# Four groups of an attention and expert block: from a loop with meetings to one list of steps

## The chip, the cores and the metric

The kernel runs on one core of a Trainium2 chip. The metric is the device time of one execution in microseconds. A NeuronCore has a matmul engine (TensorE, PE in the profile; its weight loads are shown as PEld), a vector engine (VectorE, DVE), an activation engine (ScalarE, ACT), a general engine (GpSimd, POOL) and a queue engine that issues transfers (SyncE, SP). They run side by side and wait for one another by semaphores. SBUF is the on-chip memory; PSUM, with eight banks of 128 x 512 floats, takes the results of PE.

## The reference

```python
def reference(x, Wq, bq, Wk, bk, Wv, bv, Wo, bo, gate, w1, w2, w3, c, wmod):   # x is 1 x 2048 x 128
    mod = (_silu(c) @ wmod).reshape(c.shape[0], 6, 1, -1)
    sa, ca, ga, sb, cb, gb = (mod[:, i] for i in range(6))
    ga, gb = (sign * max(abs, 0.25) of each)
    h = _layernorm(x) * (1 + ca) + sa
    x = x + ga * attn(h)     # 16 query heads, 4 key/value heads of 64, rotary, causal softmax, @ Wo + bo
    h = _layernorm(x) * (1 + cb) + sb
    x = x + gb * ffn(h)      # 8 experts 128 -> 512 -> 128, the best two of each token, silu(g) * u
    return x
```

Attention over 2048 tokens falls into four groups, one for each key/value head with its four query heads. The groups write into the same sum and are otherwise alike.

## The kernel before, in words

**Tiling.** The tokens are 16 tiles of 128 and 4 chunks of 512. A pair step J (0 to 7 within a group) is one chunk of queries for two of the four heads; chunk J // 2 sees only keys of chunks up to its own. For each pair step PE computes scores (`s`, L1039, L1041 and the mask L1044), ACT takes exponentials into `full` or, for the diagonal chunk, `diag` (L611, L620), and PE multiplies them with V (`pv`, L1058). The scores have two PSUM banks. Ahead of them the row maxima are found: PE computes scores once more (`max`, L1011, L1014), DVE reduces them (L781, L784, L790), PE transposes the result (`qmax`, L1024) and ACT copies it to QMT (L591). Projections of a tile are `proj` (PE L987, DVE's bias addition L760 and L764, the rotation on POOL L503 to L510), `low` (parts for exact products, ACT L630 to L632, DVE L770, L773) and `qk` (transposes L995, L1001, copies L591). POOL (L472, L481, L485) or DVE (L800, L811) adds up the exponentials of a pair step; its tail is six `sum` pieces (DVE L826 to L833), `rowsum` (PE L1067, DVE L837 to L840), `norm` (DVE L846) and, after each second pair step, `out`, the product with Wo (PE L1076, DVE L853). Everything but the scores and V products goes through a ring of four PSUM banks.

**Order.** All engines walk the same list of steps, in which each does its part. It is made by `group_order`: the scores and V products of the eight pair steps are laid along a line, and the other steps are placed between them by fractions of pair steps. The end of a group's list already holds projections, transposes and maxima of the next group's first two chunks (`next_group`); their values go to V_next. The beginning holds the tail of the last pair step of the group before, `tail_steps(-1)`.

**The loop.** There are three lists: the lead, which prepares group 1; the body, walked three times in a hardware loop (`Fori`); and a closing copy for group 4. All semaphore counts in a list start at zero, so at the end of the lead and of each turn every engine reports to SP (`engine_through`), SP waits for all and for all counts, clears some 20 semaphores and lets them go with `group_go` (L407, L408). The body starts on ACT with a copy of V_next into V (L648). Since the body is one for all groups, the first one has a tail of a group that does not exist: it works on ones and zeros that POOL writes at the start, with an additional slot of zero weights in `wqkv`, `bqkv` and `wo_sb`, and addresses of the group are computed from the loop's register. After the closing copy follow the second norm, the router and the experts (PE L1117, L1131), in hardware loops too.

```python
                for s, count in loop_sems(n):
                    if count:
                        sp.wait_ge(s, count)
                sp.wait_ge(engine_through, 4)
                for s, count in loop_sems(n):
                    if count:
                        sp.sem_clear(s)
                sp.sem_clear(engine_through)
                sp.sem_inc(group_go, 1)
```

Of the kernel before, what the change touches and what calls it, by code (L numbers as in the profile page):

```python
# [33 lines left out]
P = 128  # L34
# [29 lines left out]
def block_kernel(nc, x_in, Wq, bq, Wk, bk, Wv, bv, Wo, bo, gate, w1, w2, w3, c, wmod,  # L64
# [83 lines left out]
    def merge(*placed):  # L148
# [13 lines left out]
        place(tail_steps(-1), 0.02, 1.1), place(diag_steps(7), 8.01, 8.38),  # L162
# [10 lines left out]
    def group_order(*more):  # L173
        return [("values",)] + merge([(float(b), x) for b, x in zip(before, main)], [(begin[end], x) for x in pending],
                                     *side, *more)

    body = group_order(*next_group)
    closing = group_order(place(tail_steps(end - 1), 8.4, 8.9))
# [11 lines left out]

    class Counts:


        def __init__(self, order):
# [9 lines left out]
            for x in order:  # L204
                for key, engine in {
# [7 lines left out]
                                    + (x[0] == "sum" and x[1] not in range(PAIRS) and x[3] == 1)  # L213
# [9 lines left out]

    QUADS = 7
    quad_of, quad_owner = {}, []
    for x in body:
        if x[0] == "s" and x[3] == 0:
            _, J, q, _, m = x
            if q < J // PAIRS or q == 0:
                quad_of[J, m, q] = len(quad_owner)  # L230
                quad_owner.append((J, m, q))

    def acc_quad(J, m):

        J = J % N_J
        return quad_of[J, m, max(J // PAIRS - 1, 0)] % QUADS

    assert len(quad_owner) % QUADS == 0

    with ExitStack() as ctx:  # L240
# [3 lines left out]
        def sem(name):  # L244
# [11 lines left out]
        wqkv = sb("wqkv", [P, GROUPS + 1, QKV])  # L256
        bqkv = sb("bqkv", [P, GROUPS + 1, QKV])
        wo_sb = sb("wo_sb", [P, 1 + GROUPS, PAIRS, E])
# [22 lines left out]
        V = sb("V", [P, TILES, HEAD])  # L281
        V_next = sb("V_next", [P, 2 * TB, HEAD])
# [51 lines left out]
        engine_through, group_go, pads_ready, values_ready = (  # L334
            sem("engine_through"), sem("group_go"), sem("pads_ready"), sem("values_ready"))
# [14 lines left out]
        def loop_sems(n):  # L350

            k = n.number
            return [
                (proj_added, k.get("proj", 0)), (pool_chain, POOL_OPS * k.get("proj", 0)),
                (rotated_ready, k.get("proj", 0)), (pool_added, k.get("poolsum", 0)),
                (diag_added, k.get("diagsum", 0) // 2),
                (quad_added, k.get("quadsum", 0) // TB),
                (ring_filled, len(n.engine_of)), (ring_act, n.engine_of.count("act")),
                (ring_dve, n.engine_of.count("dve")), (vector_chain, n.vector_links),
                (max_ready, k.get("maxed", 0)), (scores_ready, k.get("s", 0)), (probs_ready, k.get("s", 0)),  # L360
                (pv_done, k.get("pv", 0)), (sum_ready, k.get("sum", 0) // 3),
                (attn_ready, k.get("norm", 0)), (values_ready, k.get("values", 0)),
                (parts_ready, k.get("low", 0)), (low_ready, k.get("low", 0)), (q_max_ready, k.get("low", 0)),
            ]
# [16 lines left out]
        def _(sp):  # L381
# [6 lines left out]
            sp.dma_start(wo_sb[:, 1:1 + GROUPS], Wo.rearrange("(g j p) e -> p g j e", p=P, j=PAIRS))\  # L388
# [9 lines left out]
            def end_walk(n):  # L398


                for s, count in loop_sems(n):
                    if count:
                        sp.wait_ge(s, count)
                sp.wait_ge(engine_through, 4)
                for s, count in loop_sems(n):
                    if count:
                        sp.sem_clear(s)  # L407
                sp.sem_clear(engine_through)  # L408
                sp.sem_inc(group_go, 1)
# [773 lines left out]
```

## Time and profile before

| | |
|---|---|
| median of 3 runs | 1413.32 us (1412.92 to 1414.95) |
| profiled execution | 1413.7 us, its span 1411.9 us |
| PE busy | 1305.2 us (92%), granted clock 0.966 |
| DVE busy | 926.4 us (66%) |
| ACT, POOL busy | 572.0 us (41%), 537.2 us (38%) |
| groups 1 to 4 begin on PE at | 71.39, 332.09, 592.34, 848.66 us |
| experts on PE | from 1104.74 us to the end |

The span runs from the first to the last instruction that the profiler recorded; the device time is a little longer. Busy PE is not PE at its peak, since matmuls overlap. The granted clock is a share of 2.4 GHz: 0.5 is 1.2 GHz. An idle time in brackets stands before the operation at which the engine goes on, with what released it; "issue" says that the profile shows no releaser, "SPq" is an instruction of SP's queue.

### The profile page before, as it was taken

The numbers are of one execution on the slowest core, as the hardware profiler recorded it, in microseconds if no ns is written. First come the engines' busy times: TensorE is split into PE (matmuls) and PEld (weight loads), VectorE is DVE, ScalarE is ACT, GpSimd is POOL, SyncE is SP. The second block draws the span as 40 slices with busy tenths as digits, with TensorE's granted clock in tenths as the row PEclk, the third lists the DMA queues.
The fourth block names the chain that finished last, engine by engine and source line by source line (L and its number), as shares of the span: only waits on it lengthen the run. The fifth ranks groups of instructions, "written<-read, shape, count | busy, mean of one in ns | idle before, by whom it ended". The sixth has DMA issues, their size and how long they took to land.

```text
span 1411.9 us, 18621 instructions
## 1 busy us (share of the span) xinstructions
PE 1305.2 (92%) x6752; PEld 819.6 (58%) x6752; DVE 926.4 (66%) x1786; ACT 572.0 (41%) x1184; POOL 537.2 (38%) x509
## 2 busy tenths in 40 slices
PE   3699999987999999799999979999996799999998
PEld 2455555444555554455555545555543688888887
DVE  3777877766687777677777687787666544444443
ACT  2445444534454445444534543554442323232222
POOL 4554346452364463254346354434423301010110
PEclk9799999998999999899999999999997799999999
DMA  5000000000000000000000000000001000000101
GB/s 130 1 1 1 1 1 0 1 0 2 1 1 1 0 1 0 2 1 0 1 1 0 1 0 1 1 1 0 1 1 45 1 23 24 22 22 6 36 4 30
DMA packets 18449, 13.01 MB, mean 9 GB/s; under 512 B 7105, under 2 KB 15681, under 8 KB 18369
## 3 DMA queue, kind: packets, MB, share of 16 engines
q1 hardware_dynamic: 11072, 9.58, 2.2%
q10 hardware_dynamic: 7296, 2.36, 0.7%
q8 instruction: 51, 0.84, 0.2%
q14 instruction: 30, 0.24, 0.1%
HBM read 10.88 MB, written 1.05 MB: 8 GB/s over the span
## 4 chain that ended last, share of the span: by engine, by line
PE 78%; DVE 13%; POOL 3%; issue 3%; ACT 1%; ACTq 1%; SPq 0%; DVEq 0%; POOLq 0%; another core or an unknown queue 0%
PE PS L1058 17%; PE PS L1117 12%; PE PS L1011 11%; PE PS L1039 10%; PE PS L1041 8%; PE PS L1131 8%; PE PS L1067 2%; PE PS L1076 2%; DVE part_max L784 2%; PE PS L1024 2%; DVE k_split L773 2%; DVE full L800 2%; PE PS L987 2%; PE PS L995 2%; DVE q_split L770 1%
## 5 line engine op out<-in xcount | busy, mean ns | idle before, releaser
L784 DVE TENSOR_REDUCE part_max<-PS 128x1 f32<-128x512 f32 (+2 forms) x576 | 349.0, 620 | 128.8 <-PE PS L1011 103.6
L611 ACT ACTIVATE full<-PS 128x512 f32<-128x512 f32 x384 | 224.2, 597 | 231.1 <-PE PS L1041 214.8
L1039 PE MATMUL PS<-QT,KT 128*128 128x512 f32 (+3 forms) x640 | 269.3, 421 | 17.3 <-issue 12.8
L1011 PE MATMUL PS<-KT,QT 128*128 128x512 f32 (+3 forms) x640 | 266.2, 429 | 10.0 <-ACT QMT L591 4.7
L1041 PE MATMUL PS<-QMT,KT 128*128 128x512 f32 (+3 forms) x640 | 237.1, 370 | 0.0
L472 POOL TENSOR_TENSOR full<-full 128x2048 f32<-128x2048 f32 x32 | 145.6, 4574 | 213.8 <-PE PS L1058 213.3
L1011 PEld LDWEIGHTS PS<-KT,QT 128*128 128x128 f32 x640 | 123.5, 196 | 156.2 <-DVE part_max L784 76.8
L1058 PE MATMUL PS<-full,V 128*64 128x512 f32 x768 | 209.3, 624 | 0.0
L620 ACT ACTIVATE diag<-PS 128x512 f32<-128x512 f32 (+3 forms) x256 | 111.3, 437 | 238.6 <-PE PS L1044 212.2
L1039 PEld LDWEIGHTS PS<-QT,KT 128*128 128x128 f32 x640 | 125.2, 196 | 106.9 <-issue 35.2
L906 DVE TENSOR_TENSOR full<-full,PS 128x512 f32<-128x512 f32 x128 | 87.9, 688 | 145.0 <-ACT full L668 145.0
L503 POOL TENSOR_TENSOR rot_cos<-qkv_sb,cos_sb 128x320 f32<-128x320 f32 x64 | 61.7, 964 | 293.8 <-DVE qkv_sb L760 291.5
L668 ACT ACTIVATE full<-PS 128x512 f32<-128x512 f32 x128 | 76.4, 597 | 208.7 <-PE PS L1117 208.7
L1131 PEld LDWEIGHTS PS<-full 128*128 128x128 f32 x1024 | 127.9, 191 | 7.5
L1041 PEld LDWEIGHTS PS<-QMT,KT 128*128 128x128 f32 x640 | 123.6, 193 | 13.9
L481 POOL TENSOR_TENSOR full<-full,diag 128x512 f32<-128x512 f32 (+3 forms) x128 | 107.3, 877 | 63.7 <-ACT diag L620 62.8
L1131 PE MATMUL PS<-full 128*128 128x128 f32 x1024 | 128.5, 275 | 0.0
L1117 PE MATMUL PS<-KT,QT 128*128 128x512 f32 x384 | 119.5, 420 | 6.2 <-DVE full L906 5.9
L1117 PE MATMUL PS<-KT,QMT 128*128 128x512 f32 x384 | 111.1, 398 | 0.0
L1058 PE MATMUL PS<-diag,V 128*64 128x256 f32 (+3 forms) x512 | 96.4, 457 | 0.0
L521 POOL TENSOR_TENSOR full<-full,gates 128x512 f32<-128x512 f32 x8 | 10.3, 1292 | 207.1 <-DMA full<-in_L_ffn_experts_w_dram 207.1
L1117 PEld LDWEIGHTS PS<-KT,QMT 128*128 128x128 f32 x384 | 73.5, 191 | 17.1
(116 smaller groups left out, 1661.4 us busy)
## 6 DMA issues: line engine op xcount, KB each, us to landing
full<-in_L_ffn_experts_w_dram SPq DMA_DIRECT2D x24, 256.0 KB, 3.0
out_dram<-XA SPq DMA_DIRECT2D x4, 256.0 KB, 2.3
wqkv<-in_L_attn_Wq_dram ACTq DMA_DIRECT2D x1, 512.0 KB, 4.5
bqkv<-in_L_attn_bq_dram ACTq DMA_DIRECT2D x1, 512.0 KB, 9.2
wo_sb<-in_L_attn_Wo_dram SPq DMA_DIRECT2D x1, 512.0 KB, 8.9
sin_sb<-in_k_sin_dram ACTq DMA_DIRECT2D x1, 512.0 KB, 8.8
full<-in_L_wmod_dram SPq DMA_DIRECT2D x1, 384.0 KB, 9.7
cos_sb<-in_k_cos_dram ACTq DMA_DIRECT2D x1, 256.0 KB, 9.6
```

The lines of the kernel that those rows point to most:

```text
L472: nc.gpsimd.tensor_tensor(full[:, a], full[:, a], full[:, b], ALU.add)\
L481: last = nc.gpsimd.tensor_tensor(acc[:, r, r * P:BANK], acc[:, r, r * P:BANK], diag[:, m, r, r * P:BANK], ALU.add)
L611: nc.scalar.activation(full[:, k % QUADS, r, :], PS[:, bank, :], ACT.Exp).then_inc(probs_ready, 1)
L620: nc.scalar.activation(diag[:, m, r, r * P:BANK], PS[:, bank, r * P:BANK], ACT.Exp)\
L784: nc.vector.reduce_max(part_max[:, t, b:b + 1], PS[:, bank, 0:width], AX.X).then_inc(ring_dve, 1)
L906: nc.vector.tensor_tensor(hidden[:, ch % 2, it, :], silu_g[:, u % 2, :], PS[:, 2 * (u % 2) + 1, :], ALU.mult).then_inc(hidden_ready, 1)
L1011: last = nc.tensor.matmul(PS[:, bank, 0:w], QT[:, ch % 2, h, t * P:(t + 1) * P], KT[:, 0, b * BANK:b * BANK + w], start=True, stop=not las ...
L1039: nc.tensor.matmul(o, KT[:, 0, kt * P:(kt + 1) * P], QT[:, ch % 2, h, q0:BANK], start=True, stop=False)
L1041: last = nc.tensor.matmul(o, KT[:, 1, kt * P:(kt + 1) * P], QMT[:, h, q0:BANK], start=False, stop=q < ch)
L1058: last = nc.tensor.matmul(PS[HEAD * m:HEAD * (m + 1), AV + J % 2, q0:BANK], V[:, kt, :], pT, start=(kt == 0), stop=(kt == ch * TB + TB - 1))
L1117: last = nc.tensor.matmul(PS[:, 2 * (u % 2) + m, :], w[:, b, part, it * P:(it + 1) * P], h[:, ch * BANK:(ch + 1) * BANK], start=(k == 0), ...
L1131: last = nc.tensor.matmul(PS[:, 4 + ch % 2, t * P:(t + 1) * P], hidden[:, ch % 2, it, t * P:(t + 1) * P], w2_gated[:, b, it, :], start=(it ...
```

## The change

The steps of all groups are written out as one list, with numbers that go on from group to group (`of_group`), and each engine walks it once. Semaphores are counted up over the whole list and never cleared; `end_walk`, `engine_through` and `group_go` go. The dummy tail of group 1 goes, with its zero slots and memsets. V gets eight more tiles, and the first eight tiles of every second group lie there (`values`), so that V_next, its copy and `values_ready` go. Addresses are constants. The banks of the second norm's transposes and of the router are chosen so that they don't depend on the last ring bank.

```diff
-        place(tail_steps(-1), 0.02, 1.1), place(diag_steps(7), 8.01, 8.38),
+        place(diag_steps(7), 8.01, 8.38),
...
+    def of_group(order, g):
+
+        per_group = {"proj": TILES, "low": TILES, "qk": TILES, "out": CHUNKS}
+        return [x if x[0] == "modulation" else (x[0], x[1] + g * per_group.get(x[0], N_J)) + x[2:] for x in order]
...
+    last_tail = place(tail_steps(-1), 0.02, 1.1)
+    steps = of_group(lead_in, -1)
+    for g in range(GROUPS):
+        steps += of_group(group_order(*([last_tail] if g else []),
+                                      *(next_group if g < GROUPS - 1 else [place(tail_steps(end - 1), 8.4, 8.9)])), g)
...
-        V = sb("V", [P, TILES, HEAD])
-        V_next = sb("V_next", [P, 2 * TB, HEAD])
+        V = sb("V", [P, TILES + 2 * TB, HEAD])
+
+        def values(i):
+
+            g, t = divmod(i, TILES)
+            return t + TILES if t < 2 * TB and g % 2 else t
...
-        lead, loop, last_out = Counts(lead_in), Counts(body), Counts(closing)
+        n = Counts(steps)
...
+        NORM_BANKS = ((0, 1, 2, 3), (SCORES, SCORES + 1, AV, AV + 1))
...
-            for m in range(2):
-                nc.gpsimd.memset(full[:, acc_quad(-1, m)], 1.0)
-            nc.gpsimd.memset(attnT[:], 0.0).then_inc(pads_ready, 1)
+            nc.gpsimd.memset(ones[:], 1.0).then_inc(pads_ready, 1)
...
-                    elif x[0] == "values":
-                        nc.scalar.copy(V[:, 0:2 * TB, :], V_next[:]).then_inc(values_ready, 1)
-                if ends is not None:
-                    act.sem_inc(engine_through, 1)
-                    act.wait_ge(group_go, ends)
...
-            def walk(n, g, ends):
-                known.clear()
-                for x in n.order:
-                    step(n, x, g + 1 if x[0] == "proj" and x[1] >= TILES else g)
-                pe.sem_inc(engine_through, 1)
-                pe.wait_ge(group_go, ends)
-
-            walk(lead, -1, 1)
-            with pe.Fori(0, GROUPS - 1) as g:
-                walk(loop, g, g + 2)
-            known.clear()
-            for x in last_out.order:
-                step(last_out, x, GROUPS - 1)
...
+            for x in n.order:
+                step(x)
```

How the instructions stand at the border of groups 1 and 2, on PE, before the change: the end of the loop body, and then the rows with which the body begins, which the jump returns to.

```order
L1024 MATMUL PS<-ident,q_max 128x128 [waits ring_act,max_ready]
L1024 MATMUL PS<-ident,q_max 128x128 x3
L1090 REGISTER_ALU
L1093 REGISTER_ALU [waits group_go]
L1093 COMPARE_AND_BRANCH
```

```order
L1093 UNCONDITIONAL_BRANCH [waits group_go]
L1039 MATMUL PS<-QT,KT 128x512
L1041 MATMUL PS<-QMT,KT 128x512
L1044 MATMUL PS<-causal,ident 128x128
L1011 MATMUL PS<-KT,QT 128x512
L1039 MATMUL PS<-QT,KT 128x512
```

The same place of the changed kernel on PE (there L969 is the transpose of maxima, L984 and L986 are the scores, L989 the mask, L956 the maxima's scores):

```order
L969 MATMUL PS<-ident,q_max 128x128 [waits ring_act,max_ready]
L969 MATMUL PS<-ident,q_max 128x128 x3
L984 MATMUL PS<-QT,KT 128x512
L986 MATMUL PS<-QMT,KT 128x512
L989 MATMUL PS<-causal,ident 128x128
L956 MATMUL PS<-KT,QT 128x512 [waits ring_act]
L984 MATMUL PS<-QT,KT 128x512
L986 MATMUL PS<-QMT,KT 128x512
L989 MATMUL PS<-causal,ident 128x128
L956 MATMUL PS<-KT,QT 128x128 [waits ring_act]
L959 MATMUL PS<-causal,ident 128x128
L984 MATMUL PS<-QT,KT 128x384 [waits probs_ready]
```

The matmuls keep their order; the wait and the jump between them are gone, and the maxima wait for ring banks that the group before has filled.

On DVE, at the same border, before the change, the end of the body and its beginning (L811 adds the diagonal's exponentials of pair step 7, L829 and L833 are the sums of the tail, L784 are maxima):

```order
L811 TENSOR_TENSOR full<-full,diag 128x384
L811 TENSOR_TENSOR full<-full,diag 128x256
L862 REGISTER_ALU
L865 REGISTER_ALU [waits group_go]
L865 COMPARE_AND_BRANCH
L829 TENSOR_TENSOR full<-full 128x512
```

```order
L829 TENSOR_TENSOR full<-full 128x512
L784 TENSOR_REDUCE part_max<-PS 128x1 [waits ring_filled]
L829 TENSOR_TENSOR full<-full 128x512
L833 TENSOR_TENSOR full<-full 128x512 [waits vector_chain]
L784 TENSOR_REDUCE part_max<-PS 128x1 [waits ring_filled]
```

And in the changed kernel (L769 adds the diagonal, L787 and L791 are the sums, L742 the maxima):

```order
L769 TENSOR_TENSOR full<-full,diag 128x384
L769 TENSOR_TENSOR full<-full,diag 128x256
L787 TENSOR_TENSOR full<-full 128x512 [waits diag_added]
L742 TENSOR_REDUCE part_max<-PS 128x1 [waits ring_filled]
L787 TENSOR_TENSOR full<-full 128x512
L791 TENSOR_TENSOR full<-full 128x512 [waits vector_chain]
L742 TENSOR_REDUCE part_max<-PS 128x1 [waits ring_filled]
```

DVE's work stands in the same order too; the first sum now waits for DVE's own diagonal sum in place of `group_go`. Ahead of group 1, ACT's part begins differently: before, a table load and the copy of V_next, and now the table load stands directly in front of the first exponential (L588):

```order
L561 ACTIVATE QMT<-PS 128x512 [waits ring_filled] x2
L588 ACT_TABLE_LOAD
L588 ACTIVATE diag<-PS 128x512 [waits scores_ready] x2
L588 ACTIVATE diag<-PS 128x384 [waits scores_ready] x2
L588 ACTIVATE diag<-PS 128x256 [waits scores_ready] x2
```

It is the only table load left between the lead and the second norm. PE's part has 1749 rows before the change and 3253 after it.

## Rows read from the trace of the kernel before

**Rows 1.** The page's chain of work that ended last, by engine.
```profile
PE 78%; DVE 13%; POOL 3%; issue 3%; ACT 1%; ACTq 1%; SPq 0%; DVEq 0%; POOLq 0%; another core or an unknown queue 0%
```

**Rows 2.** List of waits: engine, line, what it waited for: total us, times, longest.
```profile
PE PS L1039 <- issue: 12.8, 2, 6.7
```

**Rows 3.** Timeline, groups 1 to 2: start, us, engine, line, operation [idle before, releaser].
```profile
324.82 0.60 PE L1024 MATMUL PS<-ident,q_max 128*128 128x128 f32 x4
...
324.86 1.68 DVE L811 TENSOR_TENSOR full<-full,diag 128x512 f32<-128x512 f32 x4
...
325.10 1.12 ACT L591 ACTIVATE QMT<-PS 128x512 fp32r<-128x512 f32 x2
328.39 1.28 ACT L648 ACT_TABLE_LOAD   x1 [2.17 <-SPq L408]
...
331.03 0.69 DVE L829 TENSOR_TENSOR full<-full 128x512 f32<-128x512 f32 x1 [4.49 <-issue]
...
332.09 0.77 PE L1039 MATMUL PS<-QT,KT 128*128 128x512 f32 x1 [6.66 <-issue]
```

**Rows 4.** Timeline, groups 2 to 3.
```profile
584.03 3.30 DVE L811 TENSOR_TENSOR full<-full,diag 128x512 f32<-128x512 f32 x8
...
591.73 0.69 DVE L829 TENSOR_TENSOR full<-full 128x512 f32<-128x512 f32 x1 [4.40 <-issue]
...
592.34 0.76 PE L1039 MATMUL PS<-QT,KT 128*128 128x512 f32 x1 [6.13 <-issue]
```

**Rows 5.** Timeline, group 3 to the closing copy.
```profile
843.68 3.29 DVE L811 TENSOR_TENSOR full<-full,diag 128x512 f32<-128x512 f32 x8
...
848.57 0.62 ACT L648 COPY V<-V_next 128x512 f32<-128x512 f32 x1 [1.91 <-SPq L408]
848.60 0.69 DVE L829 TENSOR_TENSOR full<-full 128x512 f32<-128x512 f32 x1 [1.63 <-SPq L408]
...
848.66 0.49 PE L1039 MATMUL PS<-QT,KT 128*128 128x512 f32 x1 [2.81 <-SPq L408]
```

**Rows 6.** Timeline, lead to group 1.
```profile
69.00 0.66 PE L1024 MATMUL PS<-ident,q_max 128*128 128x128 f32 x4 [0.87 <-DVEq L792]
69.70 0.60 ACT L591 ACTIVATE QMT<-PS 128x512 fp32r<-128x512 f32 x1 [1.23 <-PE PS L1024]
...
71.37 0.69 DVE L829 TENSOR_TENSOR full<-full 128x512 f32<-128x512 f32 x1 [2.48 <-SPq L408]
71.39 0.47 PE L1039 MATMUL PS<-QT,KT 128*128 128x512 f32 x1 [1.73 <-SPq L408]
```

**Rows 7.** Windows, DVE's waking to L760: us, busy by engine, clock, DMA.
```profile
71.37:82.03 10.66, 10.64 (x50) 6.39 (x52) 9.15 (x17) 5.11 (x10) 0.00 (x0) 0.84 0.00 0
331.03:343.90 12.87, 11.81 (x50) 7.06 (x52) 9.26 (x16) 3.34 (x8) 0.00 (x0) 0.72 0.01 2
591.73:603.81 12.08, 11.47 (x50) 6.83 (x52) 9.26 (x17) 3.35 (x8) 0.00 (x0) 0.76 0.01 2
848.60:859.28 10.68, 10.62 (x50) 6.36 (x52) 9.24 (x16) 3.93 (x9) 0.00 (x0) 0.84 0.00 0
```

**Rows 8.** Windows, L760 to chunk 0's product, group 1; same columns.
```profile
82.03:123.23 41.20, 39.50 (x219) 22.18 (x215) 28.99 (x63) 18.81 (x46) 19.23 (x25) 1.00 0.00 1
```

**Rows 9.** Groups of instructions: sums, transpose of row sums, row sums.
```profile
L829 DVE TENSOR_TENSOR full<-full 128x512 f32<-128x512 f32 x100 | 70.6, 714 | 13.0 <-issue 8.9 <-SPq L408 4.1
...
L1067 PE MATMUL PS<-full,ones 128*64 128x512 f32 x132 | 36.2, 628 | 7.1 <-DVE full L833 7.1
...
L837 DVE STREAM_TRANSPOSE sum_cols<-PS 128x512 f32<-128x512 f32 x33 | 23.6, 715 | 34.6 <-PE PS L1067 34.5
```

**Rows 10.** DMA of 592.34 to 820 us, then of 848.66 to 1076 us.
```profile
DMA packets 13, 0.19 MB, mean 1 GB/s; under 512 B 0, under 2 KB 0, under 8 KB 0
...
DMA packets 14, 0.18 MB, mean 1 GB/s; under 512 B 0, under 2 KB 0, under 8 KB 0
```

**Rows 11.** List of waits from 1116 us on, PE's row of most time.
```profile
PE PS L1117 <- DVE full L906: 5.9, 1, 5.9
```

More of the change, by code:

```diff
@@ L173, in group_order @@
     def group_order(*more):
[L174 to L178, printed above, removed]
+        return merge([(float(b), x) for b, x in zip(before, main)], [(begin[end], x) for x in pending],
+                               *side, *more)
+    def of_group(order, g):
+        per_group = {"proj": TILES, "low": TILES, "qk": TILES, "out": CHUNKS}
+        return [x if x[0] == "modulation" else (x[0], x[1] + g * per_group.get(x[0], N_J)) + x[2:] for x in order]
     lead_in = []
@@ L212, in __init__ @@
             self.vector_links = sum((x[0] == "maxed" and x[1] % N_J >= PAIRS)
-                                    + (x[0] == "sum" and x[1] not in range(PAIRS) and x[3] == 1)
+                                    + (x[0] == "sum" and x[1] % N_J not in range(PAIRS) and x[3] == 1)
                                     + 2 * (x[0] == "rowsum")
@@ L348, in block_kernel @@
         POOL_OPS = 4
[L350 to L364, printed above, removed]
         ring_sem = {"act": ring_act, "dve": ring_dve}
-        lead, loop, last_out = Counts(lead_in), Counts(body), Counts(closing)
+        n = Counts(steps)
+        out_bank = RING + n.slot_at["out", GROUPS * CHUNKS - 1] % RING_BANKS
+        ROUTER = 4 if out_bank != 4 else 5
+        NORM_BANKS = ((0, 1, 2, 3), (SCORES, SCORES + 1, AV, AV + 1))
         NORM_PASSES = [(0, range(CHUNKS)), (1, range(CHUNKS - 1)), (1, range(CHUNKS - 1, CHUNKS))]
@@ L396, in load_expert @@
                   .then_inc(ld_w[b], 16)
[L398 to L409, printed above, removed]
-            end_walk(lead)
-            with sp.Fori(0, GROUPS - 1) as g:
-                end_walk(loop)
-            sp.wait_ge(pv_done, last_out.number["pv"])
-            sp.wait_ge(sum_ready, last_out.number["sum"] // 3)
+            sp.wait_ge(pv_done, n.number["pv"])
+            sp.wait_ge(sum_ready, n.number["sum"] // 3)
             for b in range(2):
@@ L513, in rotary @@
                 pool.sem_inc(rotated_ready, 1)
-            walk(lead, 1)
-            with pool.Fori(0, GROUPS - 1) as g:
-                walk(loop, g + 2)
-            walk(last_out, None)
+            walk()
             def gate_w2(b):
@@ L949, in _, with norm @@
             last.then_inc(mod_filled, 1)
-            def norm(n):
-                k, chunks = NORM_PASSES[n]
+            def norm(part):
+                k, chunks = NORM_PASSES[part]
                 if k == 0:
```

169 lines of the change are left out of this document (70 added, 99 removed).

## The prediction

> **What bounds the kernel now.** I read the page first: TensorE (PE) holds 78% of the chain that ended last, VectorE (DVE) 13% and "issue" 3% [rows 1]. Time has to come from stretches in which PE stands, or in which it runs at its lower clock. The list of waits then names two single stops of PE in front of L1039 with no releaser in the profile ("issue"), 12.8 us together, and next to nothing like it elsewhere on that line [rows 2]. The timeline shows where they are: at the end of each loop turn all engines meet.
>
> At the meeting of groups 1 and 2, PE's last transpose begins at 324.82 and its next matmul at 332.09, 6.66 us idle. ScalarE (ACT) goes on at 328.39 and DVE at 331.03 after 4.49 us; the reader is to see that the three wake in this order although one semaphore releases them [rows 3]. The meeting of groups 2 and 3 looks the same: 6.13 us on PE, 4.40 on DVE [rows 4]. Between group 3 and the closing copy there is a meeting but no jump back: 2.81 us on PE, 1.63 on DVE, ACT after 1.91 us [rows 5]. After the lead the last PE work ends at 69.66 and goes on at 71.39, DVE stands 2.48 us [rows 6].
>
> The windows add the second cost [rows 7]. Each begins where DVE wakes and ends where it starts the group's first bias addition (L760, at 82.03, 343.90, 603.81, 859.28). The work is the same in all four, DVE is busy for 9.15 to 9.26 us, yet they last 10.66, 12.87, 12.08 and 10.68 us at a mean granted clock of 0.84, 0.72, 0.76 and 0.84. PE comes back at half its clock (1.2 in place of 2.4 GHz) after a meeting, and the longer it stood the longer the stretch. From L760 to the end of chunk 0's product (L1076) a group takes 41.20 us at full clock; the four lie between 41.14 and 41.21 [rows 8]: what is won before L760 is kept, no later wait of a group swallows it. So I measure each meeting from the last DVE work before it to L760 behind it.
>
> **The change part by part.**
> *Meetings and jumps.* DVE's last work before the three later meetings ends at 324.86+1.68 = 326.54, 584.03+3.30 = 587.33 and 843.68+3.29 = 846.97 [rows 3 to 5]. Its next instruction will be the first sum of the group before, waiting only for DVE's own count. The idle time that goes is 4.49, 4.40 and 1.63 us.
>
> What is late next? PE's list goes straight from the last transpose to the scores. It has two score banks, so its third score matmul needs the first exponential; that needs ACT, free at 325.10+1.12 = 326.22, and the diagonal sum of its head (L811, whose second half begins at 324.86 [rows 3]). PE has over a microsecond of score and maximum matmuls before it needs that, so it stands for a few tenths at most and I expect its clock to stay up. Then DVE sets the pace of the stretch: at least its 9.26 us of work, at most the 10.68 us that the stretch took at 0.84 of the clock. I take 10.0, the middle, since single waits of DVE for PE's maxima and row sums remain. Gains: 343.90-326.54-10.0 = 7.36; 603.81-587.33-10.0 = 6.48; 859.28-846.97-10.0 = 2.31. Together 16.2 us (bounds 18.4 with 9.26, and 14.1 with 10.68).
>
> *The first group's dummy tail.* Before, the loop body also ran a tail for a group that does not exist: six sums of 0.71 us, a row sum with two transposes and a reciprocal, a normalisation, and a product with zero weights [rows 9]. In group 1 that is 4.3 us of sums and over 1.4 us of transposes on DVE ahead of L760, and 36.2 us/33 = 1.1 us of PE at L1067; the product lies behind L760, where PE has waited for GpSimd (POOL) anyway. Without it DVE has 9.15-4.3-1.4 = 3.5 us of work there, so PE's order of scores, maxima and PV sets the time: 10.64 us of busy PE, less 1.1, less the 0.16 of 10.66 us lost to the clock = 1.7, gives 7.8. Against it stands ACT: its table load of 1.28 us, which now comes in front of the first exponential. ACT is free at 70.30, so that exponential starts at 71.58 at the earliest and PE's third score waits until about 72.2, some 0.9 us. From PE's 69.66: 69.66+7.8+0.9 = 78.4, so 82.03-78.4 = 3.6 us; I take 3.5. Bounds: 1.6 if only the meeting's idle goes (1.73, less a little), 4.4 if the table load is hidden.
>
> *Edits at nothing.* The copy of V_next and the table load in front of it (1.28 us from 328.39, [rows 3]) leave ACT, where they were over before PE woke; without the meeting load and copy would cost some 1.9 us in front of the first exponential (a QMT copy of the same size is 1.12/2), so their removal is a condition of the gain rather than a gain of its own. The memsets of POOL run while the inputs load and the norm is done; without that cover they would cost their own length. The static addresses spare a few register operations. New waits across a group (ring banks, rotated_ready, attn_ready) name work that is over a microsecond old. The new banks of the last norm change no order of instructions. The section of the experts is the same.
>
> *Length of the list.* PE's list grows from 1749 to 3253 rows. The first 228 us of turn 3 moved 0.19 MB of instructions in 13 packets, the first 227 us of the closing copy, which was never run before and has no jump, 0.18 MB in 14 [rows 10], and the closing copy's 41.14 us from L760 are the shortest of the four. So every turn was fetched anew already, and straight code hides it. I cost the length at 0.
>
> Here the Trainium skill, "Runtime: NRT & Kernel Launch", section "Instruction fetch mechanics", has two rules: a taken branch out of the two pages held stalls until its page has come, and crossing a page in straight code is mostly hidden. The first fits PE's and DVE's extra time at the two jumps, not ACT's, which woke 0.3 us later than without a jump (2.17 against 1.91 us idle). By that page the meetings with a jump lose more than the one without, as the rows have it, and the sum would be the same.
>
> **Sum.** 16.15 + 3.5 = 19.65 us. The profiled execution had a span of 1411.9 and 1413.7 us in all; so 1392.3 and 1394.0. The median of the runs shown, 1413.32, is 0.4 below that execution: 1393.7 us.
>
> **The rivals.**
> *A, only the idle time returns.* PE's clock falls at a group's start as before, because small stops of PE at the end of a group remain (about a microsecond each) and the table load stops it in group 1. Against it: behind the meeting with the shortest stop but one, L1039 still took 0.49 us, where it took 0.76 us behind a jump [rows 4, 5], so the clock was full up to there in spite of them, and fell after the stop. Then the gain is DVE's idle time alone, 4.49+4.40+1.63 = 10.5, and 1.6 to 2.5 at the first: 12 to 13 us, 1400.3 to 1401.2.
> *B, the jump of the expert loop is laid badly.* The loops of the experts remain, and their code now starts elsewhere in memory. Before, PE had one wait in that whole section, 5.9 us where it begins, and none at the jumps [rows 11]. If a jump there cost what a jump cost the group loop over the plain meeting, 6.66-2.81 = 3.85 us, three turns take 11.6 us of the gain: about 1405.
> *C, slower: straight code stalls.* If PE's longer list had to wait for code as after a jump, 3.85 us each, six such stops would turn the gain into a loss of 3.5 us, 1417 us. It decides from the sixth stop on. Against it speaks all of the closing copy, where the trace has no such stop [rows 10]. The skill's page just named says of such crossings "mostly hidden", which is no bar to a few that are not.
> *D, no change.* The stretches behind L760 would have to give back what the meetings gave: the phase of POOL against DVE shifts, say, and DVE waits beside POOL's long additions more often. The equal stretches of all groups speak against it [rows 8]. 1413 us.
>
> **How the numbers follow.** Forecast 1393.7 with chance 0.62, its own range 1390 to 1397; A 0.20; B 0.06; C 0.04; D 0.04; more gain than all terms' bounds (18.4+4.4 = 22.8, so under 1390.5), as where group ends shorten too, 0.04. Between 1389 and 1402 lie the forecast, A and most of the last. 0.2% is 2.8 us, about what a measurement tells from none. Faster by more: 0.62+0.20+0.06+0.04 = 0.92; within: 0.04; slower: 0.04.
>
> **What would show it.** Right: PE's stop between the last L1024 of a group and the next group's first score under 1 us; DVE's first sum directly behind L811; from there to L760 about 10 us at a granted clock near 1.0; 41.2 us from L760 to the first product; group 1 reaches L760 about 9 us after the last transpose of the lead. Wrong: "issue" stops of some microseconds inside the groups or at the expert loop (C, B), a clock of 0.5 at group starts (A), or a longer time from L760 on (D).

## The result

The changed kernel takes 1390.81 us (median of 4 runs, 1389.94 to 1394.40); the kernel before took 1414.13 us on the same chip (4 runs). The ratio is 0.984, with a 95% interval of 0.9821 to 0.986. The forecast was 1393.7, which is 19.65 us below the 1413.32 shown before. The median fell by 23.3 us, the profiled execution by 22.8 (1413.7 to 1390.9), its span by 22.9 (1411.9 to 1389.0).

In the lines below, before's L760 (bias addition) is L720, L811 (diagonal sums) L769, L829 and L833 (sums of the tail) L787 and L791, L1024 (transposes) L969, L1039 (first score matmul) L984, L1067 (row sums) L1012, L1076 (output product) L1021, and L770 and L773 (splits) L728 and L731. The page of the changed kernel, its totals and its chain by engine, which answers to [rows 1]:

```profile
span 1389.0 us, 18379 instructions
PE 1294.5 (93%) x6732; PEld 812.5 (58%) x6732; DVE 919.5 (66%) x1775; ACT 567.2 (41%) x1178; POOL 532.4 (38%) x503
q8 instruction: 46, 0.75, 0.2%
q14 instruction: 30, 0.25, 0.1%
PE 77%; DVE 14%; issue 3%; POOL 3%; ACT 1%; ACTq 1%; DVEq 0%; POOLq 0%
```

The two queues that carry instructions move no more than before, with a list nearly twice as long on TensorE (PE).

The timeline of the changed kernel at the border of groups 1 and 2, PE first, then VectorE (DVE), which answers to [rows 3]:

```profile
319.84 1.06 PE L969 MATMUL PS<-ident,q_max 128*128 128x128 f32 x8
320.66 0.48 PE L984 MATMUL PS<-QT,KT 128*128 128x512 f32 x1
320.98 0.40 PE L986 MATMUL PS<-QMT,KT 128*128 128x512 f32 x1
...
327.67 1.08 PE L1012 MATMUL PS<-full,ones 128*64 128x512 f32 x4 [1.29 <-DVE full L791]
...
318.73 3.29 DVE L769 TENSOR_TENSOR full<-full,diag 128x512 f32<-128x512 f32 x8
321.95 0.68 DVE L787 TENSOR_TENSOR full<-full 128x512 f32<-128x512 f32 x1
322.56 0.68 DVE L742 TENSOR_REDUCE part_max<-PS 128x1 f32<-128x512 f32 x1
...
331.19 0.48 DVE L720 TENSOR_TENSOR qkv_sb<-PS,bqkv 128x320 f32<-128x320 f32 x1
```

Nothing in brackets stands behind L984: PE goes from the last transpose into the scores, and the matmul takes 0.48 us, full clock, where it took 0.76 after the stop. DVE begins the sums of the group before right behind L769 and has no idle time up to L720: 331.19 - (318.73 + 3.29) = 9.17 us. The other two borders give 9.16 and 9.16. PE's one stop is now 1.29 us at L1012, for DVE's sums.

The windows of 12 us over the three borders (us, busy by engine, granted clock, DMA), which answer to [rows 7]:

```profile
322.00:334.00 12.00, 10.71 (x65) 6.58 (x65) 10.87 (x22) 3.06 (x8) 2.17 (x4) 1.00 0.00 0
575.00:587.00 12.00, 10.70 (x66) 6.64 (x66) 10.47 (x21) 2.86 (x7) 2.57 (x4) 1.00 0.00 1
827.00:839.00 12.00, 10.70 (x65) 6.40 (x64) 11.07 (x22) 3.27 (x8) 1.97 (x4) 1.00 0.00 1
```

The clock is 1.00 where it was 0.72, 0.76 and 0.84 behind these borders. And the start of group 1, PE and then ScalarE (ACT), which answers to [rows 6]:

```profile
69.40 0.66 PE L969 MATMUL PS<-ident,q_max 128*128 128x128 f32 x4 [0.86 <-DVEq L750]
69.81 0.48 PE L984 MATMUL PS<-QT,KT 128*128 128x512 f32 x1
...
72.65 0.44 PE L984 MATMUL PS<-QT,KT 128*128 128x384 f32 x1 [1.05 <-ACT diag L588]
...
70.70 1.28 ACT L588 ACT_TABLE_LOAD   x1
72.00 1.09 ACT L588 ACTIVATE diag<-PS 128x512 f32<-128x512 f32 x2
...
78.61 0.49 DVE L720 TENSOR_TENSOR qkv_sb<-PS,bqkv 128x320 f32<-128x320 f32 x1
```

The table load stands in front of the first exponential and PE waits 1.05 us for it, as foretold (0.9). From the first score to the bias addition the mean clock is 1.00 here too.

Where the time came from can be read off one landmark in the chain of work, the output product of each group's chunk 0 [rows 8]. It begins 3.48 us earlier in group 1 (123.23 to 119.75), 12.75 in group 2 (385.11 to 372.36), 20.03 in group 3 (645.00 to 624.97), 22.85 in group 4 (900.42 to 877.57). The section of the experts adds nothing: the last product of attention is 22.84 us earlier and the span 22.9. So up to these four landmarks 3.5, 9.3, 7.3 and 2.8 us were gained. Not all of it is the borders'. From that product to DVE's last diagonal addition group 1 is 1.0 us shorter than it was (203.31 to 202.27 us; this 1.0 is in the 9.3), and groups 2 and 3 are 0.05 and 0.3 longer (202.22 and 201.97 to 202.27 and 202.26). The 1.0 us is the clock's: behind a stop of 5.0 us that both kernels have near the end of group 1 (see the runs on GpSimd below), PE's clock was back at 1.00 about 6 us after PE went on in the kernel before, and about 4 us after it in the changed one.

### The profile page after: what moved, and what is told of

Read it like the earlier page. It is cut to its first block, busy times and chain, and to the rows that moved or that the text cites. A ratio compares the mean times of both kernels' runs of the same rounds, so it can differ in the third digit from the quotient of the medians.

```text
span 1389.0 us, 18379 instructions
## 1 busy us (share of the span) xinstructions
PE 1294.5 (93%) x6732; PEld 812.5 (58%) x6732; DVE 919.5 (66%) x1775; ACT 567.2 (41%) x1178; POOL 532.4 (38%) x503
## 3 DMA queue, kind: packets, MB, share of 16 engines
HBM read 10.88 MB, written 1.05 MB: 9 GB/s over the span
## 4 chain that ended last, share of the span: by engine, by line
PE 77%; DVE 14%; issue 3%; POOL 3%; ACT 1%; ACTq 1%; DVEq 0%; POOLq 0%
PE PS L1002 17%; PE PS L1050 12%; PE PS L956 10%; PE PS L984 10%; PE PS L1064 8%; PE PS L986 8%; DVE part_max L742 2%; PE PS L1021 2%; PE PS L1012 2%; PE PS L969 2%; DVE k_split L731 2%; DVE full L758 2%; PE PS L933 2%; DVE full L787 2%; PE PS L940 2%
## 5 line engine op out<-in xcount | busy, mean ns | idle before, releaser
L742 DVE TENSOR_REDUCE part_max<-PS 128x1 f32<-128x512 f32 (+2 forms) x576 | 348.8, 620 | 130.0 <-PE PS L956 104.1
L956 PE MATMUL PS<-KT,QT 128*128 128x512 f32 (+3 forms) x640 | 263.5, 425 | 9.5 <-ACT QMT L561 5.0
L984 PE MATMUL PS<-QT,KT 128*128 128x512 f32 (+3 forms) x640 | 266.6, 417 | 1.1 <-ACT diag L588 1.1
L986 PE MATMUL PS<-QMT,KT 128*128 128x512 f32 (+3 forms) x640 | 234.4, 366 | 0.0
L956 PEld LDWEIGHTS PS<-KT,QT 128*128 128x128 f32 x640 | 121.7, 193 | 155.8 <-DVE part_max L742 78.8
L588 ACT ACTIVATE diag<-PS 128x512 f32<-128x512 f32 (+3 forms) x256 | 111.3, 438 | 227.9 <-PE PS L989 202.6
L984 PEld LDWEIGHTS PS<-QT,KT 128*128 128x128 f32 x640 | 123.2, 193 | 90.8 <-ACT diag L588 32.1
L986 PEld LDWEIGHTS PS<-QMT,KT 128*128 128x128 f32 x640 | 121.8, 190 | 13.4
```

Of the source, the lines that this page charges most:

```text
L588: nc.scalar.activation(diag[:, m, r, r * P:BANK], PS[:, bank, r * P:BANK], ACT.Exp)\
L742: nc.vector.reduce_max(part_max[:, t, b:b + 1], PS[:, bank, 0:width], AX.X).then_inc(ring_dve, 1)
L956: last = nc.tensor.matmul(PS[:, bank, 0:w], QT[:, ch % 2, h, t * P:(t + 1) * P], KT[:, 0, b * BANK:b * BANK + w], start=True, stop=not las ...
L984: nc.tensor.matmul(o, KT[:, 0, kt * P:(kt + 1) * P], QT[:, ch % 2, h, q0:BANK], start=True, stop=False)
L986: last = nc.tensor.matmul(o, KT[:, 1, kt * P:(kt + 1) * P], QMT[:, h, q0:BANK], start=False, stop=q < ch)
```

## The experiments

The question was what in a meeting costs. Before, a meeting is four things at once: a report of each engine and one release, SyncE's (SP's) wait until every counter shows finished work, some 20 clears of counters, and a jump back. Each run below is the median, and its ratio is to the kernel before on the same chip. The runs were made on three chips, on which the kernel before took 1413.65, 1413.91 and 1413.55 us, so a difference of a few tenths between runs says nothing.

**Straight code with the meetings kept.** The group loop of before is written out, and a spare count that nobody reads follows each wait; nothing else changes.

```
-            with sp.Fori(0, GROUPS - 1) as g:
+            for g in range(GROUPS - 1):
...
+                    act.sem_inc(passed, 1)
```

> The kernel before with its three loop turns written out, all else kept: meetings, clears, dummy tail, V_next. Theory: the jump itself costs what the two borders behind a turn lost over the border without a jump, counted from the end of DVE's last work to L760: 17.36-12.31 = 5.05 us and 16.48-12.31 = 4.17 us. So 9.2 us less than before, 1404 to 1406 us, with every border near 12.3 us. Rival: the meeting is slow at these borders for another reason (SP's waits and clears in its own loop), and the jump of the engines costs nothing: no change, 1412 to 1416 us.

Measured: 1405.84 us, ratio 0.9944 (0.9927 to 0.996). At the border of groups 1 and 2, DVE and PE of this kernel:

```profile
326.72 0.69 DVE L832 TENSOR_TENSOR full<-full 128x512 f32<-128x512 f32 x1 [1.56 <-SPq L409]
326.72 0.76 PE L1043 MATMUL PS<-QT,KT 128*128 128x512 f32 x1 [2.70 <-SPq L409]
...
584.34 0.47 PE L1043 MATMUL PS<-QT,KT 128*128 128x512 f32 x1 [3.22 <-SPq L409]
```

DVE stands 1.56 us where it stood 4.49 with the jump, PE 2.70 where it stood 6.66 [rows 3]; at the next border (last line) 2.09 and 3.22 where they were 4.40 and 6.13 [rows 4]. The loop and its jump back were worth 7.8 us (1413.65 - 1405.84), within the range expected; "nothing" is out. Written-out code also has constant addresses and, at two borders, no table load on ACT, so 7.8 us is the price of the loop as a whole.

The borders did not come out alike, though. From DVE's last addition to the bias addition they take 13.57, 12.69 and 11.31 us, where some 12.3 was expected of each and they were 17.36, 16.48 and 12.31. The first two gained 3.8 us each. The third gained 1.0 although no jump had stood there: this time PE's clock stayed up behind it. PE still wakes at half clock at the first border (0.76); at the second it wakes at full clock (0.47) after the longer stop and falls to half within 2 us.

**The same without the dummy tail.** The tail of a group that does not exist is left out of group 1; it changes no output.

> The same written-out kernel, and group 1 without the tail of a group that does not exist. Theory: with the meeting kept, ACT's table load and copy of V_next come before the first exponential, PE waits for them, and the tail is worth only 0.5 to 1.5 us: 1403 to 1405 us. Rival: the dummy tail is the main part of the 3.5 us that the first border gave: 3 us or more under the written-out kernel with the tail, 1401 to 1402 us.

Measured: 1404.65, ratio 0.9935 (0.9918 to 0.9952). The 1.2 us less are what was expected, but the runs of the two kernels overlap (1404.92 to 1407.36 against 1403.72 to 1405.83), and the trace does not show the gain at its place. PE's third score of group 1:

```profile
73.89 0.69 PE L1045 MATMUL PS<-QT,KT 128*128 128x384 f32 x1 [0.76 <-ACT diag L624]
```

From PE's first score of group 1 to the bias addition this execution takes 11.20 us (71.34 to 82.54) and the one with the tail 10.64 (70.24 to 80.88). Without the tail PE has to wait for the exponential behind ACT's table load, and then runs at half clock up to about 80 us. What made the kernel faster in all lies in great part at the border of groups 1 and 2, where PE was at half clock for a shorter time (12.17 us against 13.57). What the dummy tail itself costs is not shown.

**The changed kernel with plain meetings.** Four reports and a release at each border, no waiting for finished work, no clears, no jump.

```
+            for g in range(1, GROUPS + 1):
+                sp.wait_ge(engine_through, 4 * g)
+                sp.sem_inc(group_go, 1)
...
+            engine.sem_inc(engine_through, 1)
+            engine.wait_ge(group_go, k)
+            engine.sem_inc(passed, 1)
```

> The changed kernel with a plain meeting put back at the four borders (all engines report, SP lets them go; no clears, no jump, counters still rise). Theory: a meeting costs at the borders of groups what the border without a jump lost over the changed kernel, 12.31-9.17 = 3.1 us, and at the lead's end some 2 us, less a few tenths each since nothing is cleared: 8 to 11.5 us more, 1399 to 1402.5 us. Rival: the clears by SP are most of a meeting, the report and release alone is under 1 us each and leaves the clock up: 1392 to 1395 us.

Measured: 1390.90, ratio 0.9845 (0.9827 to 0.9863), the time of the changed kernel. My theory (1399 to 1402.5) fell, and the rival (1392 to 1395) was too dear as well. The timeline of this kernel at the border of groups 1 and 2 shows why, PE and then DVE:

```profile
320.62 0.47 PE L1005 MATMUL PS<-QT,KT 128*128 128x512 f32 x1 [0.24 <-SPq L412]
...
318.23 3.29 DVE L788 TENSOR_TENSOR full<-full,diag 128x512 f32<-128x512 f32 x8
321.44 0.68 DVE L806 TENSOR_TENSOR full<-full 128x512 f32<-128x512 f32 x1
```

PE is released at 320.62, though DVE's additions ahead of its report last until 321.52. The report is a bare count in the engine's list, and it was made while the additions in front of it were still under way. A meeting that asks only "have you come this far in your list" stops nobody for more than 0.24 us here, and DVE reaches the bias addition in 9.16 us at all three later borders, as in the changed kernel.

**Plain meetings with PE kept busy.** As before, and PE makes 24 transposes in each meeting, which adds work whose result nobody reads.

> The kernel with plain meetings, and PE does 24 transposes of the unit matrix into a score bank between its report and its wait (added work, some 3 us, thrown away). Theory: some 1.5 us of each border is the half clock of PE after the stop; kept busy, PE stays at full clock and each border costs only DVE's idle time of 1.3 to 1.6 us plus what the added work overhangs: 3 to 6 us less than with idle meetings, 1394 to 1398 us, granted clock 1.0 behind each border. Rival: the slow stretch behind a meeting comes from queues that have run empty, not from the clock: no less than with idle meetings.

Measured: 1399.37, ratio 0.9896 (0.988 to 0.9913), slower than the plain meeting where I expected it faster. Since the plain meeting had no stop to fill, this says nothing on the clock: the transposes delay the scores and DVE waits for them. It shows only that PE's time right behind a border is not free: the four fillers of 2.78 us cost 8.5 us together, and DVE idles 1.75 us behind each later border for PE's results.

**Waiting for finished work.** The changed kernel with meetings in which SP first waits for the counters of finished work.

```
+                for s, count in done_sems(g):
+                    if count:
+                        sp.wait_ge(s, count)
```

> The changed kernel with a meeting put back at each of the four borders, in which SyncE first waits until the counters of all finished work stand at their values of the border, and then for the four reports; no counter is cleared. The plain meeting before (reports alone) cost nothing: 1390.9, and the trace shows TensorE 0.24 us and VectorE not at all idle there, so the reports came before the engines' queued work was through. In the straight-line run with meetings and clears the engines did stop: VectorE 1.56 us after its last addition at the border of groups 1 and 2, TensorE 2.70. Theory A, that waiting for finished work makes the stop and the clears lengthen it: stops of about 0.3 us on VectorE and 1.3 us on TensorE at each border, and a part of the half clock behind it: 1394 to 1399. Rival B, that the clears alone are what stopped the engines: 1390 to 1392. Rival C, that the waiting is all of it: 1402 to 1405.

Measured: 1396.74, ratio 0.9875 (0.9859 to 0.9892): theory A. At the border of groups 1 and 2, DVE and PE of this kernel:

```profile
325.10 0.69 DVE L823 TENSOR_TENSOR full<-full 128x512 f32<-128x512 f32 x1 [0.35 <-SPq L429]
325.10 0.47 PE L1022 MATMUL PS<-QT,KT 128*128 128x512 f32 x1 [1.48 <-SPq L429]
```

DVE, last to finish, loses 0.35 us, PE 1.48, the same at all three later borders; the clock stays full there (0.47). From DVE's waking to the bias addition it is now 9.75 us, against the 9.16 of the changed kernel from the end of the same addition: released together with DVE, PE no longer has a start on it, and DVE idles 0.4 us for PE's maxima. That makes 0.93 us a border, 2.8 for the three.

The whole price is higher, 5.9 us by the medians, 6.1 by the profiled spans. In the profiled execution 0.3 us more lies at the first meeting and the rest mostly in places with the same work: inside group 1 the clock fell behind an idle time of 1.45 us (1.5 us lost there) and was slower to come back behind the 5.0 us stop (0.9), and at the start of the experts its mean over 19.5 us was 0.65 where it was 0.70 (1.0). Why the clock does this more often in this kernel is open.

**And the clears.** SP clears a spare counter 20 times ahead of the release.

```
+                for _ in range(20):
+                    sp.sem_clear(scratch)
```

> As the run before, and SyncE clears a spare counter 20 times ahead of the release, as many clears as the kernel before makes. Theory: this gives the cost of the straight-line meetings back without their copy of V and their dummy tail: VectorE stopped about 1.6 us and TensorE about 2.7 us at each border, and half clock for some 7 us after it: 1402 to 1405 (the straight-line run with meetings was 1405.8, and 1404.65 without the dummy tail). Rival, that only real counters or the copy of V matter: within 1 us of the run without clears.

Measured: 1404.83, ratio 0.9929 (0.9912 to 0.9946), as the theory had it. With straight meetings, no jump and no dummy tail the earlier run had 1404.65: the time is reproduced without the copy of V. PE and DVE of this kernel at the border of groups 1 and 2:

```profile
328.25 0.76 PE L1025 MATMUL PS<-QT,KT 128*128 128x512 f32 x1 [2.64 <-SPq L431]
328.25 0.69 DVE L826 TENSOR_TENSOR full<-full 128x512 f32<-128x512 f32 x1 [1.51 <-SPq L431]
```

Windows of it behind the next two borders:

```profile
584.00:590.00 6.00, 4.97 (x15) 3.22 (x15) 3.74 (x7) 1.69 (x3) 0.00 (x0) 0.50 0.01 3
841.00:847.00 6.00, 5.42 (x30) 3.32 (x30) 4.95 (x9) 2.48 (x5) 0.00 (x0) 1.00 0.00 1
```

DVE's stop grows from 0.35 to 1.51 us, 1.16 for 20 clears; at the next two borders it is 2.02 and 1.50 (why the middle one is longer is not known). The clears cost more than these 4.0 us, 8.1 us over four meetings, because the longer stop can take PE's clock: from DVE's waking to the bias addition it is 10.55, 11.71 and 9.75 us at the three later borders, where PE starts at half, half and full clock. Against the 9.75 us at full clock that is 0.8, 2.0 and 0 us, 2.8 together.

**The same stop with PE kept busy.** PE makes 20 transposes between its report and its wait.

> As the run with clears, and TensorE runs 20 transposes of 128 columns between its report and its wait, some 2.3 us at 0.116 us each (24 took 2.78 us in an earlier run), within the stop that it has anyway. Theory, that about half of what a stop costs is the half clock behind it (VectorE's idle time behind the stop was 2.6 us in the straight-line run against none in the changed kernel): the granted clock stays at 1.00 over the borders and the time falls by 1 to 1.5 us a border: 1397 to 1401. Rival, that the clock costs nothing since VectorE's list bounds the stretch: the same time as the run with clears, within 1 us.

Measured: 1400.92, ratio 0.9907 (0.9891 to 0.9924). The filler's row, the matmul and DVE's addition behind it, and then the window over them:

```profile
323.44 2.35 PE L1074 MATMUL PS<-ident 128*128 128x128 f32 x20
326.24 0.47 PE L1025 MATMUL PS<-QT,KT 128*128 128x512 f32 x1 [0.45 <-SPq L431]
326.24 0.69 DVE L826 TENSOR_TENSOR full<-full 128x512 f32<-128x512 f32 x1 [1.51 <-SPq L431]
```

```profile
324.00:332.00 8.00, 7.50 (x48) 4.96 (x46) 6.01 (x12) 3.24 (x7) 0.00 (x0) 1.00 0.01 2
```

DVE stands 1.51 us as before (2.02 and 1.50 at the next two), PE's clock stays at 1.00, and all three borders take 9.75 us from DVE's waking. More work on PE, 3.9 us less time: that is the clock's share, shown by itself. It is 1 us a meeting on average, the low end of what I expected, but not 1 us at each: 1.2 at the first, then 0.8, 2.0 and 0. The profiled executions differ by 5.5 us, since the one with clears also had a fall of the clock inside group 1 (10.31 us between the second and third bias addition) and this one had none (8.77).

**What bounds the groups now: GpSimd (POOL) against DVE.** The trace of the changed kernel shows one large loss that both kernels have, once in each of groups 1 to 3. The places are the splits of projections, DVE additions with both inputs in SBUF. DVE and then PE in group 1:

```profile
291.30 4.74 DVE L728 TENSOR_TENSOR q_split<-rotated,q_split 128x256 fp32r<-128x256 f32 x1 [0.32 <-ACT k_split L599]
295.97 4.52 DVE L731 TENSOR_TENSOR k_split<-rotated,k_split 128x64 fp32r<-128x64 f32 x1
304.67 0.22 DVE L731 TENSOR_TENSOR k_split<-rotated,k_split 128x64 fp32r<-128x64 f32 x1
...
301.20 1.12 PE L969 MATMUL PS<-ident,q_max 128*128 128x128 f32 x4 [5.04 <-DVEq L750]
301.97 0.78 PE L984 MATMUL PS<-QT,KT 128*128 128x512 f32 x1
```

L731 takes 0.22 us elsewhere and 4.52 here; POOL runs two additions of 2048 columns at that time, 9.20 us together. L728's median in the whole kernel is 0.56 us (the expectation below gives 0.68 us for both lines, which is too much). PE then stands 5.04 us and comes back at half clock. I cut POOL's addition into four pieces, and in a later run into two.

```
-                            nc.gpsimd.tensor_tensor(full[:, a], full[:, a], full[:, b], ALU.add)\
-                              .then_inc(pool_added, 1)
+                            for r in range(TB):
+                                last = nc.gpsimd.tensor_tensor(full[:, a, r], full[:, a, r], full[:, b, r], ALU.add)
+                            last.then_inc(pool_added, 1)
```

> The changed kernel with GpSimd's additions of 2048 columns made as four of 512. In groups 1 to 3 VectorE's additions L728 and L731, 0.68 us each otherwise, take 4.7 and 4.5 us while GpSimd's additions of 4.57 us run (294.79 and 299.45 in the trace of before), and TensorE then idles 5.0 us. Theory, that VectorE is held until the one GpSimd instruction ends: held by pieces of 1.15 us it takes about 1.2 us instead, 6 to 7 us come back in each of three groups: 1369 to 1375. Rival, that it is the traffic of both on the same memory that slows VectorE, however it is cut: 1389 to 1392.

> The changed kernel with GpSimd's additions of 2048 columns made as two of 1024, some 2.35 us each. Theory, that VectorE's addition waits for the end of the one GpSimd instruction under way: the two waits in each group shrink from 4.7 us to about 2.4 us, where four pieces brought them to 1.3 to 1.5; two thirds of the 18.7 us that four pieces brought come back, 12 to 14 us: 1377 to 1379. Rival, that each GpSimd instruction more costs time of its own, or that any cut brings it all: 1372 or less, or over 1385.

Measured: four pieces 1372.11, ratio 0.9704 (0.9688 to 0.9721); two pieces 1377.62, ratio 0.9753 (0.9738 to 0.9768); both as the theory had it. Between the two bias additions around this place it is 13.34 us in the changed kernel, 9.03 with two pieces and 6.85 with four, which three groups make into most of the 13.2 and 18.7 us. The splits beside the pieces, first with four (POOL's row ahead), then with two:

```profile
290.16 10.32 POOL L449 TENSOR_TENSOR full<-full 128x512 f32<-128x512 f32 x8 [0.18 <-POOL rotated L484]
...
290.26 1.46 DVE L729 TENSOR_TENSOR q_split<-rotated,q_split 128x256 fp32r<-128x256 f32 x1 [0.32 <-ACT k_split L600]
291.65 1.31 DVE L732 TENSOR_TENSOR k_split<-rotated,k_split 128x64 fp32r<-128x64 f32 x1
292.88 0.68 DVE L740 TENSOR_REDUCE q_max<-PS 128x1 fp32r<-128x512 f32 x1
```

```profile
290.61 9.54 POOL L449 TENSOR_TENSOR full<-full 128x1024 f32<-128x1024 f32 x4 [0.18 <-POOL rotated L485]
...
290.71 2.57 DVE L730 TENSOR_TENSOR q_split<-rotated,q_split 128x256 fp32r<-128x256 f32 x1 [0.32 <-ACT k_split L601]
293.20 2.38 DVE L733 TENSOR_TENSOR k_split<-rotated,k_split 128x64 fp32r<-128x64 f32 x1
```

DVE's addition lasts as long as one POOL instruction: 4.60 (9.20/2), 2.39 (9.54/4) or 1.29 us (10.32/8) of POOL give 4.52, 2.38 and 1.31 on DVE. That is a hold until the other's instruction ends, not two engines sharing a rate. The Trainium skill, "SBUF — State Buffer", section "SBUF: two separate sides", states it so: VectorE and GpSimd share one pair of ports as an exclusive lock, held for the whole instruction, and a VectorE operation with two inputs in SBUF needs it when the GpSimd instruction reads SBUF. The trace agrees, down to the reduction from PSUM (L740), which takes its usual 0.68 us in the middle of POOL's pieces. The eight pieces take 10.32 us in place of 9.20; POOL has that time.

**The table load made early.** One exponential of one column, read by nobody, ahead of ACT's list; alone, and with the four pieces.

```
+            nc.scalar.activation(warm[:], ones[:, 0:1], ACT.Exp)
```

> The changed kernel with an exponential of one column ahead of ScalarE's list, so that the load of the function table (1.28 us at 70.70 in the trace after, ahead of group 1's first exponential) is made while ScalarE has nothing else to do. TensorE idles 1.05 us behind that load. Theory: this idle time goes and nothing takes its place: 0.9 to 1.1 us less than the changed kernel's 1390.8, so 1389.8. Rival: VectorE's list bounds the stretch up to the bias add and nothing is gained: 1390.8.

> GpSimd's additions in four pieces and the early table together. Theory, that the two gains add up: 1372.1 less 1.0 = 1371.1. Rival, that the early table is worth nothing: 1372.1.

Measured: 1390.38 (1389.94 to 1393.00), ratio 0.9842 (0.9829 to 0.9856), and 1372.58, ratio 0.9715 (0.9702 to 0.9728). Neither can be told from its kernel without the load. Locally the gain is there: from PE's last transpose of the lead to the bias addition it is 77.31 - 70.01 = 7.30 us, and 78.61 - 70.06 = 8.55 without. In the profiled execution of the first it was lost again at once. Windows of that kernel, then the same stretch of the changed kernel:

```profile
84.00:86.00 2.00, 1.99 (x10) 1.21 (x11) 1.46 (x3) 0.98 (x2) 2.00 (x5) 0.96 0.00 0
86.00:88.00 2.00, 2.00 (x8) 0.71 (x7) 1.41 (x5) 1.29 (x4) 1.36 (x3) 0.50 0.00 0
88.00:90.00 2.00, 2.00 (x10) 1.18 (x8) 0.68 (x2) 0.24 (x1) 0.00 (x0) 0.68 0.00 0
```

```profile
86.00:88.00 2.00, 2.00 (x12) 1.09 (x12) 1.79 (x4) 1.51 (x4) 1.92 (x5) 1.00 0.00 0
```

Behind an idle time of 1.45 us, which both kernels have in front of the same matmul (84.01 and 85.31), the clock fell in the one execution and not in the other. By the fourth bias addition the lead of 1.3 us was a lag of 0.2 (100.48 against 100.25). With the four pieces the clock did not fall there, and still the spans were equal (1370.4 and 1370.2). That gain too went to the clock: the experts began 0.8 us earlier than without the early load (1062.72 against 1063.52) and took 1.0 us more, for the same work, with a mean clock of 0.65 against 0.73 over their first 19.5 us. These are single executions; that the early load brings such falls about is not shown.

## Why the prediction held

**The mechanism: right, and now taken apart.** PE's stop, the half clock behind it and DVE's wait were gone at all borders. By medians the runs divide the gain so: the loop with its jump back 7.8 us, the clears with the clock that they cost 8.1, waiting for finished work 5.9, and 1.2 between the runs with and without the dummy tail, which no trace puts at the tail; the plain meeting and the copy of V nothing that can be measured. That these add up to 23.0 is no proof, since they are the steps of one way from 1413.65 down to 1390.81; what is tested in it is that two kernels built differently, with waits and clears alike, take 1404.65 and 1404.83. And each step carries what the clock happened to do. The prediction had the plain meeting and its parts in one lump ("each meeting from the last DVE work before it to L760 behind it"), which gave a good size but not its cause.

**The number: in the range, but at its edge.** 1390.81 lies 0.8 us inside the range of 1390 to 1397, and the gain was 23.3 us by the medians where 19.65 was added up. Nearly all of the difference is one term.

**The borders: 16.15 us foretold, 18.66 found.** This term was mis-sized, by "I take 10.0, the middle, since single waits of DVE for PE's maxima and row sums remain". None remained: DVE took 9.17, 9.16 and 9.16 us. From 17.36, 16.48 and 12.31 us before, the gains were 8.19, 7.32 and 3.15, more together than the bound of 18.4 that the prediction gave. That bound took DVE's 9.26 us of busy time for the least possible, but rows that follow one another without a wait overlap a little: the sum at 321.95 lasts 0.68 us and the reduction begins 0.61 us after it, and the busy time of the stretch is now 8.88 us. And the waits did not remain because PE no longer starts together with DVE: its first score begins at 320.66, 1.3 us before DVE's first sum. Where a meeting releases both at once, 0.4 us of such waits come back even at full clock (9.75 us).

**The first group: 3.5 foretold, 3.42 found** (82.03 to 78.61). PE was held by the table load as written. The lead ended 0.4 us later in this execution, so the stretch itself gave 3.8: 2.0 of idle time before the first score (1.73 us, and 0.25 by which the score now starts before the last transpose ends), and 1.8 behind it (10.64 to 8.80). How much of the 1.8 is the tail and how much the clock (0.84 to 1.00) was not taken apart.

**Edits at nothing, length of the list: right.** The two instruction queues carried the same, no "issue" stop stands in front of the score matmuls, and the section of the experts took as long as before, so rivals B and C did not come. The stretches behind the bias addition kept what the borders gave, so D did not come either; over the four groups the landmark moved by 3.48 + 9.27 + 7.28 + 2.82 = 22.85.

**Rival A** (the clock falls all the same) failed at all four starts, where the clock is 1.00. But the clock is not as sure as the prediction made it: in group 1, behind an idle time of 1.45 us, it fell in the profiled executions of the runs with waiting, with clears and with the early table load, and not in that of the changed kernel. Runs of the changed kernel reach from 1389.94 to 1394.40, and such a fall costs some 1.5 us; that the spread is made of such falls is not shown.

**Jumps.** The prediction laid the longer stops at the two jumps to fetched code. The Trainium skill, "Runtime: NRT & Kernel Launch", section "Instruction fetch mechanics", says a taken branch out of the held pages stalls. The runs agree for PE and DVE: without the jump 4.49 and 6.66 became 1.56 and 2.70. That the time went into fetching was not measured apart from the rest of the loop.

## What to carry to other kernels

Report and release alone cost nothing measurable here; what cost was waiting for work to be finished, bookkeeping done one by one while all stand, the loop with its jump, and the clock that TensorE can lose by standing. One list with counters that only rise does away with the first three. Price each by the time from the last work of the pacing engine to its next fixed landmark, not by the idle time alone. When the change is in, look for DVE additions that take ten or twenty times their length beside a long GpSimd instruction: cutting that instruction into four gave 18.7 us here, nearly as much as the whole change, for three lines.

## What the hardware showed that was not expected

- A bare count in an engine's list came ahead of the end of the engine's running work: PE was released 0.9 us before DVE's additions in front of the report were through (320.62 and 321.52).
- 20 clears on SP lengthened the stop by 1.16 us, some 58 ns each, at two borders, and by 1.67 us at the one between them; with the clock, the time grew by 2.0 us a meeting.
- The granted clock does not answer to the length of a stop alone: after 2.63 us it stayed at 2.4 GHz once (third border, run with clears), after 2.64 it was 1.2 GHz, after 3.22 (straight meetings, second border) PE woke at 2.4 GHz and fell within 2 us, after 1.48 it stayed up, and after 1.45 in group 1 it fell in one execution and not in another.
- How fast the clock comes back differs too: behind the same 5.0 us stop in group 1 it took about 6 us in the kernel before and 4 in the changed one, which alone is 1.0 us.
